# Turned softmax results through VectorE and DRAM instead of TensorE, and output products behind the next pair's scores

## The reference, cut to what matters

```python
h_q = (x @ w_q.T).reshape(b, lq, H, DH)          # b 8, lq 128, H 32, DH 128
h_k = (key_value_states @ w_k.T).reshape(b, lk, H, DH)
h_v = (key_value_states @ w_v.T).reshape(b, lk, H, DH)
score = jnp.einsum('bqhd,bkhd->bhqk', h_q, h_k) + position_bias[None]
score = jnp.where(m, score, -jnp.inf)
score = jnp.where(m, jax.nn.softmax(score, axis=-1), 0.0)
attn = jnp.einsum('bhqk,bkhd->bqhd', score, h_v).reshape(b, lq, H * DH)
out = attn @ w_out.T
```

## Time and profile before

| | us |
|---|---|
| median of 3 runs | 924.41 (923.97 to 925.29) |
| profiled execution | 923.94 |
| its span | 922.2 |
| PE busy | 873.8 |
| DVE busy | 627.6 |
| ACT busy | 424.1 |
| POOL busy | 353.1 |

### The profile page before, as it was taken

The page is one execution under the profiler, slowest core; times in us unless marked ns, Lnnn a source line. Parts: engine busy times, 40 slices in busy tenths (PEclk is TensorE's granted clock), DMA queues, the critical chain, the costliest instruction groups (busy, mean ns, idle before and its releaser), DMA issues.

```text
span 922.2 us, 14534 instructions
## 1 busy us (share of the span) xinstructions
PE 873.8 (95%) x4528; PEld 732.2 (79%) x4528; DVE 627.6 (68%) x1086; ACT 424.1 (46%) x1091; POOL 353.1 (38%) x328
## 2 busy tenths in 40 slices
PE   4789998999999999988999999999999999999898
PEld 4677786887677888767888888888888888888697
DVE  6877775677876666566557766676657766676654
ACT  3553344566434435264545453555445553554220
POOL 2312333333443323152764355534464355533100
PEclk9999999999999999999999999999999999999999
DMA  8025665555666767607244442535234441533002
GB/s 273 12 92 136 160 138 137 138 149 137 151 149 158 202 159 138 143 20 193 74 121 116 117 114 79 142 91 142 82 112 122 111 128 68 139 91 68 1 1 92
DMA packets 207661, 108.27 MB, mean 117 GB/s; under 512 B 136592, under 2 KB 187920, under 8 KB 203920
## 3 DMA queue, kind: packets, MB, share of 16 engines
q1 hardware_dynamic: 207632, 107.91, 44.7%
HBM read 74.34 MB, written 33.55 MB: 117 GB/s over the span
## 4 chain that ended last, share of the span: by engine, by line
PE 80%; DVE 10%; issue 3%; POOL 2%; DMA 2%; ACT 2%; SPq 1%; DVEq 0%; ACTq 0%; POOLq 0%
PE bank L575 63%; PE bank L629 6%; PE bank L647 6%; PE bank L639 3%; DVE w_lo L1259 2%; DVE turned L1351 2%; DVE st L1268 1%; DMA values<-turned 1%; PE bank L593 1%; SPq L337 1%; DVE stats L1152 1%; DMA acc<-in_x 1%; POOL w_sum L479 1%; POOL rstd L458 1%; DVE acc L1145 1%
## 5 line engine op out<-in xcount | busy, mean ns | idle before, releaser
L955 ACT COPY st<-bank 128x512 f32<-128x512 f32 x192 | 112.2, 587 | 266.5 <-PE bank L575 260.0
L575 PE MATMUL bank<-ctx_hi,w_hi 128*128 128x512 f32 x448 | 179.7, 401 | 15.6 <-DVE st L1268 7.8
L1268 DVE TENSOR_TENSOR st<-bank,st 128x512 f32<-128x512 f32 x144 | 98.6, 689 | 125.4 <-PE bank L575 125.3
L575 PE MATMUL bank<-ctx_hi,w_lo 128*128 128x512 f32 x448 | 175.4, 391 | 0.0
L575 PE MATMUL bank<-ctx_lo,w_hi 128*128 128x512 f32 x448 | 175.3, 391 | 0.0
L477 POOL TENSOR_TENSOR w_sum<-raw 128x256 f32<-128x256 f32 x48 | 39.6, 825 | 248.8 <-PE bank L575 224.3
L536 POOL TENSOR_TENSOR probs<-probs,row_scale 128x512 f32<-128x512 f32 x64 | 66.6, 1041 | 177.3 <-DVE row_scale L1233 174.3
L575 PEld LDWEIGHTS bank<-ctx_hi,w_hi 128*128 128x128 f32 x448 | 84.4, 188 | 45.5 <-issue 11.0
L575 PE MATMUL bank<-wo_hi,ot_hi 128*128 128x512 f32 x256 | 104.9, 410 | 5.4 <-issue 3.6
L1145 DVE TENSOR_TENSOR acc<-bank,acc 128x512 f32<-128x512 f32 x136 | 93.6, 690 | 20.6 <-PE bank L575 18.7
L901 ACT ACTIVATE probs<-probs,neg_max 128x128 f32<-128x128 f32 x264 | 102.4, 393 | 1.1 <-DVE neg_max L1217 1.1
(11 more groups left out here) (135 smaller groups left out, 1520.2 us busy)
## 6 DMA issues: line engine op xcount, KB each, us to landing
raw<-in_weights SPq DMA_DIRECT2D x128, 256.0 KB, 3.1
values<-turned SPq DMA_DIRECT2D x64, 256.0 KB, 4.3
v<-values SPq DMA_DIRECT2D x64, 256.0 KB, 4.5
keys<-st SPq DMA_DIRECT2D x14, 1024.0 KB, 4.8
st<-keys SPq DMA_DIRECT2D x14, 1024.0 KB, 7.4
acc<-in_x SPq DMA_DIRECT2D x8, 256.0 KB, 7.6
ctx_raw<-in_ctx_t SPq DMA_DIRECT2D x4, 512.0 KB, 9.9
bias<-in_pos_bias SPq DMA_DIRECT2D x16, 128.0 KB, 2.0
```

Of the source, the lines that this page charges most:

```text
L575: ins = pe.matmul(out_ap, lhs[a], rhs[b], start=start and k == 0, stop=stop and k == n - 1, skip_group_check=again)
L955: act.copy(to[:, i, j, :], (y, other, y, y)[which][:, :]).then_inc(act_took, 1)
L1268: dve.tensor_tensor(to[:, i, j, :], (other, y, other)[which][:, :], to[:, i, j, :], ALU.add).then_inc(dve_took, 1)
```

## The change

- The softmax results of heads of pairs 0 to 14 are no longer turned on PE. POOL writes the normalised halves to new tiles `weighed[0]`, `weighed[1]`; DVE turns their 32x32 blocks (`turn_probs`, two transposes of 128x512 per head) back into `probs[j]`; SP stores the tile to DRAM (`store_blocks`, 512 KB in rows of 4 KB) and loads it back with four DMAs (`load_probs_t`, 128 KB each, runs of 1 KB) into `probs_t[j]`, of which there are now two, one for each head.
- The last pair's two heads are still turned on PE, into the banks QK (`turn_last_probs`, `copy_last_probs`).
- PE weighs head 0 of pair g-1 between slots 3 and 4 of pair g, and no longer at the end of pair g-1. The eight output products use banks VO, TO, SC, VO in turn.
- On DVE the last two `low_for_queries` of pair g+1 move from pair g to the head of pair g+1.
- SP's list is in another order, with query weights fetched two pairs ahead, and the weights of the feed-forward part at the end of `refill(1)`. Their cast on ACT and their low part on POOL are cut in four (`FFN_PARTS`), one a pair; ACT's first quarter stands at the end of pair 1.

```diff
+        OUT = VO + TO + SC + VO
...
-            def refill(g, last=False):
-                if not last:
-                    sp.wait_ge(w_lo_ready[0], 4 * (Q_USE + g) + 4)
-                    fetch_heads(0, g + 1, Q_COLS)
-                    fetch_bias(g + 1)
+            def store_blocks(g, j):
+                sp.wait_ge(blocks_turned, 2 * (PAIR * g + j) + 2)
+                sp.dma_start(by_blocks[j].rearrange("a k c n -> (a k) (c n)"),
+                             by_block[j].rearrange("p c b q -> p (c b q)")).then_inc(blocks_stored[j], 16)
+            def load_probs_t(g, j):
+                sp.wait_ge(blocks_stored[j], 16 * g + 16)
+                if not isinstance(g, int) or g:
+                    sp.wait_ge(pv_done, 2 * PAIR * g + 2 * j)
+                for c in range(4):
+                    sp.dma_start(probs_t[j][cols(c, QUAD), :, :, :].rearrange("k a b q -> k a (b q)"),
+                                 by_blocks[j, :, :, c, :].rearrange("a k n -> k a n")
+                                 ).then_inc(probs_t_loaded[j], 16)
+            def fetch_queries(g):
+                sp.wait_ge(w_lo_ready[0], 4 * (Q_USE + g))
+                fetch_heads(0, g, Q_COLS)
+            def refill(g, first=False, ahead=2):
                 sp.wait_ge(pv_done, 2 * PAIR * g + 2)
                 load_values(g)
-                if not last:
-                    sp.wait_ge(scores_done, 2 * PAIR * g + 6)
-                    load_keys(g + 1)
-                    sp.wait_ge(wo_lo_ready, g + 1)
-                    fetch_out(g + 1)
+                store_blocks(g, 0)
+                load_probs_t(g, 0)
+                next_keys(g + 1)
+                store_blocks(g, 1)
+                if ahead == 2:
+                    fetch_queries(g + 2)
+                load_probs_t(g, 1)
+                next_out(g + 1)
+                if ahead == 2:
+                    fetch_bias(g + 2)
+                if first:
+                    fetch_ffn()
...
-                    pool.tensor_tensor(probs[j][:, half(i), :], probs[j][:, half(i), :],
+                    pool.tensor_tensor(weighed[i][:, :, :], probs[j][:, half(i), :],
...
-            def pair(g, first=False):
+            def pair(g, first=False, last=False):
                 project_queries(g, range(4))
-                turn_head_probs(g - 1, 1)
+                weigh_head_values(g - 1, 0)
                 project_queries(g, range(4, SLOTS))
...
                 weigh_head_values(g - 1, 1)
                 pe.wait_ge(act_took, 4 * (FIRST + g) + 4)
                 head_scores(g, 1)
-                project_out(g - 1, range(6))
-                turn_head_probs(g, 0)
-                project_out(g - 1, (6, 7))
-                weigh_head_values(g, 0)
+                if last:
+                    project_out(g - 1, range(6))
+                    turn_last_probs(0)
+                    project_out(g - 1, (6, 7))
+                else:
+                    project_out(g - 1)
...
-                copy_probs_t(PAIR * g + 1, probs_t)
+                if last:
+                    copy_last_probs(0)
                 act.wait_ge(out_done, B * (g + 1))
                 high_out(g)
-                split_head_out(g, 0)
-            pair(1)
-            act.wait_ge(ffn_loaded, 48)
-            act.copy(ffn[0][:, :], ffn_raw[:, :]).then_inc(ffn_hi_ready, 1)
+                if then is not None:
+                    then()
+            def high_ffn(i):
+                act.wait_ge(ffn_loaded, 48)
+                at = cols(i, ffn_cols // FFN_PARTS)
+                act.copy(ffn[0][:, at], ffn_raw[:, at]).then_inc(ffn_hi_ready, 1)
+            for g in range(1, 1 + FFN_PARTS):
+                pair(g, lambda: high_ffn(g - 1), first=g == 1)
...
+            def turn_probs(g, j, i):
+                if i == 0:
+                    dve.wait_ge(probs_ready, 2 * (PAIR * g + j + 1) + 2)
+                dve.transpose(by_block[j][:, :, half(i), :].rearrange("p c b q -> p b c q"),
+                              weighed[i][:, :, :].rearrange("p b (c q) -> p b c q", c=4)).then_inc(blocks_turned, 1)
```

More of the change, by code:

```diff
@@ L22 @@
 QUAD = 32
+FFN_PARTS = 4
 NE, NR = 8, 16
@@ L555, in pair @@
                     add_mask(g + 1, 1)
-            pair(1)
-            pool.wait_ge(ffn_hi_ready, 1)
-            pool.tensor_tensor(ffn[1][:, :], ffn_raw[:, :], ffn[0][:, :].bitcast(F32),
-                               ALU.subtract).then_inc(ffn_lo_ready, 1)
-            with pool.Fori(2, GROUPS - 1) as g:
+            for g in range(1, 2 + FFN_PARTS):
+                pair(g, (lambda: low_ffn(g - 2)) if g > 1 else None)
+            with pool.Fori(2 + FFN_PARTS, GROUPS - 1) as g:
                 pair(g)
@@ L705, in project_out @@
-            def project_out(g, some):
+                if not last:
+                    pe.wait_ge(probs_t_loaded[j], 64 * g + 64)
+                pe.wait_ge(ot_lo_ready, 2 * s)
+                if j == 0:
+                    pe.wait_ge(out_added, B * g + HALF)
+                for i in range(2):
+                    if last:
+                        pe.wait_ge((probs_t0_copied, probs_t1_copied)[i], 1 + j + 1)
+                    for t in range(HALF):
+                        b = HALF * i + t
+                        ins = pe.matmul(TO[i][:, cols(t)], v[:, j, b, :], probs_t[j][:, :, b, :], start=True, stop=True)
+                    ins.then_inc(pv_done, 1)
@@ L1076, in _, with pair @@
             take(K1, 1, kt)
[L1077 removed]
+            exponentials(1, 0, probs[0], 1)
             take(K1, 2, kt)
[L1079 removed]
             high_for_queries(1, (0, 1))
+            exponentials(2, 1, probs[1], 0)
             take(K1, 3, kt)
             high_for_queries(1, (2, 3))
[L1083 to L1085 removed]
             exponentials(2, 1, probs[1], 1)
[L1087 to L1089 removed]
+            def pair(g, then=None, first=False, last=False):
                 n = FIRST + g
@@ L1095, in pair @@
                 take(n, 2, qt)
-                copy_probs_t(PAIR * g, probs_t)
+                if first:
+                    high_out(0)
+                split_head_out(g - 1, 0)
                 take(n, 3, qt)
@@ L1489, in pair @@
                     maxima(PAIR * g + 2, 1, probs[1], i)
-                for b in range(B):
-                    add_out(g, b)
-                    if b < 2:
-                        row_scales(g, 0, b)
-                    elif b in (2, 3, 4, 6) and not last:
-                        low_for_queries(g + 1, (2, 3, 4, 6).index(b))
-                    if b in (4, 5):
-                        row_scales(g, 1, b - 4)
-                    if b == 5:
-                        copy_probs_t(PAIR * g + 1, probs_t)
-                split_head_out(g, 0)
-            with dve.Fori(1, GROUPS - 1) as g:
+                row_scales(g, 0, 0)
+                row_scales(g, 0, 1)
+                add_out(g, 0)
+                add_out(g, 1)
+                if not last:
+                    turn_probs(g, 0, 0)
+                    turn_probs(g, 0, 1)
+                add_out(g, 2)
+                if not last:
+                    low_for_queries(g + 1, 0)
+                add_out(g, 3)
+                row_scales(g, 1, 0)
+                row_scales(g, 1, 1)
+                add_out(g, 4)
+                if not last:
+                    low_for_queries(g + 1, 1)
+                add_out(g, 5)
+                if last:
+                    copy_last_probs(0)
+                else:
+                    turn_probs(g, 1, 0)
+                    turn_probs(g, 1, 1)
+                add_out(g, 6)
+                add_out(g, 7)
+            pair(1, first=True)
+            with dve.Fori(2, GROUPS - 1) as g:
                 pair(g)
             pair(GROUPS - 1, last=True)
-            copy_probs_t(HEADS, probs_t)
+            split_head_out(GROUPS - 1, 0)
+            copy_last_probs(1)
             split_head_out(GROUPS - 1, 1)
```

172 lines of the change are left out of this document (114 added, 58 removed).

## The result

The changed kernel takes 926.34 us, median of 20 runs (921.06 to 932.11); the kernel before, run 20 times on the same chip, 923.03 (918.34 to 925.66). The ratio is 1.0042, 95% interval 1.0022 to 1.0062: some 0.4% slower, where 915 us and a gain of 1% were predicted. The profiled execution of the changed kernel took 922.49 us with a span of 920.7, so it lies 3.9 us under the median.

The account below looks back on a forecast made before the run. PE was taken to bound the pair loop. 922.2 - 27.6 - 7.3 - 1.5 + 6.5 + 17.5 + 2.6 = 912.4 us of span, so 915 us, 1% faster; range 905 to 927, the forecast's own 910 to 921.

Parts of the forecast that it names:

- The transposes: PE, pair loop: 31 groups of eight transposes removed from its path at 0.89 us each, -27.6 us.
- Six banks: PE's output products rotate over six banks instead of two: 0.1 us x 14, -1.5 us.
- The small items: Four small waits or slow stretches on PE's path go, together -7.3 us.
- The waits of 3.62, 0.87 and 1.12 us: PE: the wait at 426.37, the one for takes and the lack from 440 to 630 all go.
- the half clock at 427: PE's half-clock stretch over 427 to 431, behind the 3.62 us wait, goes: 1.7 us.
- the first part: Time to the first pair's start of output products: the prediction's terms there make -5.4 us.
- Slot 3: Next query products: PE waits 0.5 us for w_lo, held by GpSimd's low_out, in 13 pairs, +6.5 us.
- The FFN weights: Pair 2: PE waits once for ScalarE's cast of late-landing FFN weights, +17.5 us, bounds 13 and 20.
- the half clock behind it: PE runs at half clock behind the wait for the FFN weights, +1.7 us.
- Rival B: The FFN weights don't stop PE, the transfer being covered as before: 896 us; chance 7%.
- the way through DRAM of head 1: Head 1's store and loads land before PE weighs it: cover of 1.7 us, counted as 0.
- rival C: Head 1's loads land late in each of 14 pairs; 936 us at 1.5 us beyond cover; chance 17%.

Follow-up runs that it names:

- run 20: Not a label of a run: the kernel before was run 20 times on the same chip, 923.03 us.
- e6: e4 with sixteen transposes of the identity, results unread, put back on PE in each of pairs 1 to 14: 913.20 us, ratio 0.988.
- e5: The kernel before, with the FFN weights fetched behind the query weights and bias of refill(1): 919.80 us, ratio 0.995.
- e3: The changed kernel with both the edits of e1 and e2: 896.92 us, ratio 0.971.
- e4: e3 with VectorE's last two w_lo of the next pair moved back between the output products' additions: 888.65 us, ratio 0.962.
- e9: The changed kernel with only the last two w_lo of the next pair moved between the output products' additions: 908.95 us, ratio 0.983.
- e1: The changed kernel with ScalarE's casts of the FFN weights and GpSimd's low parts one pair later: 907.64 us, ratio 0.983.
- e2: The changed kernel with head 1's loads issued ahead of the next query weights on SP: 917.31 us, ratio 0.993.
- e11: e8 without the edit of e2, so SP's order of loads is the changed kernel's: 892.27 us, ratio 0.963.
- e8: e7 with GpSimd's second mask addition moved behind the first normalise where the heads begin: 888.68 us, ratio 0.962.
- e7: e4 with the FFN weights fetched in three parts behind refills 1, 2 and 3, cast from pair 4 on: 889.32 us, ratio 0.962.
- e10: The changed kernel with both the edits of e1 and e9, SP's order left as it is: 888.34 us, ratio 0.961.

## Why the prediction was wrong

**The transposes, right.** 0.89 us for a group was predicted, 0.92 measured (e6: 1.83 for two). **Six banks, right**: products of 10.99 us against 11.0 (0.1 us x 14 is 1.4, where the sum has 1.5). **The small items, in part.** The waits of 3.62, 0.87 and 1.12 us and the half clock at 427 are gone, as forecast; 4.6 us of that could be had without the change (e5). New is a wait of 2.24 us where the heads begin, with a clock of 0.83 over 400 to 410, which is 1.7 us where 0.9 was forecast. That the first part still came out 1.7 us better than forecast proves no term, since the start of the heads varies by 6 us.

**Slot 3, right.** 0.5 us a pair was forecast, for w_lo held by GpSimd's low_out; e3 has periods of 28.2, e4, which differs by the two w_lo alone, of 27.70: 0.5 us. The Trainium skill (GPSIMD Engine Reference, Specifications) has the two engines contend for the shared interface when a VectorE instruction has two SBUF inputs. These runs agree: the two w_lo took 2.47 and 2.86 us beside GpSimd, and 0.92 and 0.64 in e9, where GpSimd is at work for under 0.4 us of each. Block transposes, with one input, took 0.66 to 0.71 us with GpSimd at work all through (24 of them in the changed kernel's stage of keys and values) and 0.66 to 0.72 with none.

**The FFN weights, right.** Behind the first products' end (430.22) the last landing was predicted at 19.3 us and came at 20.5; PE's wait was to be 17.5 us and was 19.0; the half clock behind it cost 2.4 us, not 1.7. The whole was to cost 19.2 us, and e1's first period puts it at 20.4 (49.14 - 28.76). Rival B (no stop) is thereby out.

**The step that failed is the way through DRAM of head 1: "Cover of 1.7 us; counted as 0".** In the text's own measure (E, the products' end) the loads should be issued from 7.6 and land by 11.9, at worst 13.9, and PE should weigh at 13.6. PE was ready at 13.75 (as e2 shows: 661.05 behind an end at 647.31). But the loads were issued at 8.3, and PE's weighing began between 13.6 and 15.0; in seven of the thirteen pairs the trace names the loads as what it waited for. 0.7 us of it is SP's late issue: the last w_lo, held by a mask addition as the one before it is by wo_lo, keeps `raw` from being overwritten until 7.1 (6.7 forecast). The larger part is landing time: I had taken about 2.3 us from a row of transfers without neighbours; with 512 KB of query weights just ahead of them, in twelve of the pairs, the four loads of a pair took 3.2 to 3.9 us in their median and 3.5 to 5.0 in their slowest.

The cost: periods of 28.82 us in the mean against e2's 28.22, 0.6 us in each of thirteen, 7.8 us together. That is nearly all of the 8.3 us between the forecast span (912.4) and the measured (920.7); the other misses are smaller and of both signs, and nearly cancel. This is rival C, "loads land late", given 17%, at its near end: it put the turn from faster to slower at 0.7 us beyond the cover. That 926.3 lies within 905 to 927 is owed to the width of that range; it lies outside the forecast's own, 910 to 921.

**What this step should have looked at.** Both ends were in the rows: 128 KB in 2.0 us, and a landing of 8.0 us for 256 KB issued into a queue. I carried only the low end into the sum where SP's order puts 512 KB directly in front, though even the worst case written down, 13.9, lay beyond PE's 13.6.

**Open.** Of the 11.7 us between the forecast 914.6 and the measured 926.3 the span holds 8.3. The other 3.4 lie between the profiled execution and the median (3.9 us here, 0.5 forecast), and with them the sign: the profiled executions differ by -1.5 us, the medians by +3.3. The changed kernel's mean granted clock doesn't explain them: eight runs with 0.983 have spans of 919.2 to 925.9. Nor do loads that are later in other executions: e2 has none late, its median is 4.0 us above its profiled run all the same, and it gained 9.0 us in the median where the profiled spans differ by 9.2. The four kernels whose last two w_lo are held (the changed one, e1, e2, e3) have medians 3.9 to 5.1 us above their profiled runs; where these are early it is anything from 5.2 below to 3.6 above. Whether the w_lo make the difference no trace shows, with one profiled execution of each kernel, so the cause of these 3.4 us stays open.

## What to carry to other kernels

A transfer whose cover is 1 to 2 us is not covered until everything that its queue issues just ahead of it has been counted, bytes included; take its landing from rows with such neighbours (here 2.9 us with the neighbours 6 us ahead, 3.9 with them 1 us ahead). When an engine's work moves into DMAs, ask what each of these issues waits for on its queue, back to the last instruction that frees a buffer: here two subtractions on VectorE, held by GpSimd, delayed SP's issues and PE's slots. Moving them gave 10.8 us in the profiled spans and 17.4 in the medians (e9), as much as the transposes of six to ten pairs (1.83 us a pair). And a one-time load put at the end of a refill needs its first readers moved as well: moving them one pair on gave 18.7 us (e1).

## What the runs showed of the hardware that was not expected

**Half clock outlasts the wait, and is not certain.** Around the 19 us wait PE's clock was 0.50 from about 436 to 457, five of them with work. At the end of the last pair PE waits 2.58 or 2.59 us in every one of the thirteen traces, with the same matmuls behind it, and the clock behind it differs. The windows of e11 and of e8, whose last pairs end in the same way at 840:

```profile
840.00:855.00 15.00, 15.00 (x70) 14.32 (x71) 7.04 (x17) 3.69 (x6) 1.21 (x2) 0.54 0.00 0
```
```profile
840.00:855.00 15.00, 14.50 (x104) 13.33 (x105) 10.38 (x26) 5.86 (x11) 1.21 (x2) 1.00 0.00 0
```

In e11 the clock was 0.50 from 842 to 854 with PE busy all the time. From the wait to the end e11 took 52.6 us (892.6 - 840.0), e8 46.5 (886.8 - 840.3). Of the other eleven traces five have full clock there too and take 46.4 to 46.5 us, six have 0.89 or 0.90 over the first 15 us and take 47.4 to 47.7. So the same wait costs nothing, 1 us or 6 us, and 6 us is more than the medians of e7, e8, e10 and e11 differ by. The runs of e11 follow their mean clock (spans 892.6 and 892.5 at 0.985, 890.6 at 0.988, 886.5 at 0.992, 885.8 at 0.994), and those of the kernel before likewise, 918.1 at 0.996 to 926.6 at 0.985; at which place these other runs lose their clock is not shown.

**GpSimd pays too.** Its two mask additions took 4.74 us and 4.72 in e9, but 5.63 beside the held w_lo. Each of the two takes some 2.83 us and not 2.37, and each starts (684.58, 687.37) while a w_lo that had been held still runs, to 685.17 and 687.96.

**A late DMA can find its cover again.** e6 put 1.83 us into each of fourteen pairs, and its span grew by 5 us less than that, mainly since the wait of e4's one bad pair is gone. The medians don't show such a gain (24.6 of 25.6 us), so it holds for these two executions.
